# Block scales of a decoded FFN weight: the engine that multiplies them

## The chip, the cores and the metric

The kernel runs on one core of one Trainium2 chip. The metric is device time in microseconds (us). The kernel before took 1120.23 us (median of 3 runs, 1119.17 to 1120.62).

## What is computed

Two layers over x of 32 x 64 x 1024 (2048 rows of 1024), all float32:

```python
x = x + _L0_ffn_ref(_L0_cond_ref(x, L0_cond_weights, itok_B_0_15), L0_ffn_lora_A, L0_ffn_lora_B, L0_ffn_W, L0_ffn_bias, L0_ffn_lora_weights)
x = x + _L1_ffn_ref(_L1_cond_ref(x, L1_cond_A, L1_cond_B, itok_B_3_7), L1_ffn_gate_codes, ..., L1_ffn_down_scales)
```

Layer 0 picks a 64x64 channel matrix by sample, then a linear 1024x1024 with LoRA and bias. Layer 1 picks a rank 16 adapter pair by sample (8 pairs), and then runs a gated FFN with hidden size 2752, whose three weight matrices are stored as 4-bit codes with a scale for each block of 64:

```python
def dequant_nf4(codes, scales):
    out_dim, in_dim = codes.shape
    vals = NF4[codes].reshape(out_dim, in_dim // BLOCK, BLOCK)
    return (vals * scales[:, :, None]).reshape(out_dim, in_dim)
inter = jax.nn.silu(gate) * up
return jnp.einsum('bsi,hi->bsh', inter, Wd)
```

The last multiplication of `dequant_nf4`, by the block's scale, is what this document is about.

## The kernel before

**Units.** The three code matrices are cut into 65 units of 128 x 1024 codes: 21 of gate, 21 of up, 22 of down (the last one half as wide) and one tail of gate and up together. A unit n is decoded in three buffers `val` in turn. ScalarE makes eight lines (L502 the first, into `val`; L506 seven more, into a ring of five buffers), straight lines in the code. VectorE merges the seven into `val` by minimum or maximum (L666, L668), and then multiplies by the block scales (L685). These eight VectorE instructions are the steps 8n to 8n+7; 8n+7 is the scale. It raises the semaphore `scaled`, on which TensorE's `turn_unit` (L885) waits: it transposes the unit into PSUM (`ps_t`), ScalarE copies it out (gate and up into `wt`, L518; down into `wd_..._hi`, L529), and gate and up units are multiplied by the adapter A (`adapter_ga`, L893), copied out (`ga_f`, L541, semaphore `ga_evac`) and split by GpSimd into a high and a low part (`split_ga`, L417 and L419).

**Stages.** After a setup (to about 58 us) the first stage loops over 16 row tiles t: layer 0 and the adapter input Bx for the tile (L840, L851, L860, L868), with one or two units turned for each t (22 in all). The second stage loops over 6 groups of hidden chunks and, in each, over 16 slots (row tiles): down products (L972), gate and up products for the next block (L956), and up to one unit turned at the end of a slot. Group 0 has only two chunks. The result of a slot is evacuated (`staged`, L619, semaphore `out_evac`) and added to the output in memory by a GpSimd DMA (`accumulate`, L478).

**Order.** All queues are written out by hand. How many steps VectorE does in each t or slot is in `STEPS_A` and `STEPS_SLOT` (L126); ScalarE's lines run `LEAD` = 4 steps ahead. VectorE does in a slot: `product` (L786), one step, `inter_lo` (L792), `low_wd` (L703, a subtraction), the rest of the steps. GpSimd does in each t: `store_x1` of the tile before (L404), `split_ga` of the second unit of the t before, `split_bx` (L440, L442), `split_ga` of this t's first unit, `load_conds` (L398); in each slot: `split_ga` of the unit turned in the slot before, and `accumulate` of the slot before. TensorE in a t: half of `ffn_z`, `turn_x1`, `ffn_z`, `cond_y`, `adapter_ga` of the second unit of the t before, `turn_unit`, `ffn_z` and the rest. Each engine does its list strictly in order.

Of the kernel before, what the change touches and what calls it, by code (L numbers as in the profile page):

```python
# [10 lines left out]
ALU = mybir.AluOpType  # L11
# [22 lines left out]
COMBOS = len(MERGES)  # L34
# [15 lines left out]
def adaln_ffn(nc, x, cond_id, adapter_id, cond_w, lora_a, lora_b, w0, bias0, lora_w, ad_a, ad_b,  # L50
# [3 lines left out]
    P = 128  # L54
    ROWS = SAMPLES * CH
    NT = ROWS // P
    PER = P // CH
    DC = D // P
# [5 lines left out]
    BLK = D // gate_scales.shape[1]  # L64
    SB = gate_scales.shape[1]
    DSB = down_scales.shape[1]
    FULL = HID // P
    REM = HID - FULL * P
    TAIL = FULL
    NB = ROWS // HALF  # L70
    TPB = HALF // P
# [12 lines left out]
    UNITS = [(kind, c) for c in range(10) for kind in "gu"]  # L84
# [27 lines left out]
    NU = len(UNITS)  # L112
# [8 lines left out]
    STEPS = COMBOS + 1  # L121
    STEPS_SETUP = 12
    STEPS_A = [11 if t < 10 else 10 for t in range(NT)]
    LEAD = 4
    LINES_AT = [STEPS_SETUP + LEAD + sum(STEPS_A[:t]) for t in range(NT + 1)]
    STEPS_SLOT = [[4, 4, 3, 4]] + [[5, 4, 5, 4]] * (NG - 3) + [[5, 5, 5, 5], [0, 0, 0, 0]]  # L126
# [4 lines left out]
    with ExitStack() as ctx:  # L131
        def sb(name, shape, dt, where=ctx):
            return where.enter_context(nc.sbuf_tensor(name, shape, dt))

        def sem(name):
            return ctx.enter_context(nc.semaphore(name))
# [3 lines left out]
        d_scales = sb("d_scales", [P, DC, DSB], F32)  # L140
        gu_scales = sb("gu_scales", [P, FULL + 1, 2, SB], F32)
# [67 lines left out]
        gu_scales_in = sem("gu_scales_in")  # L209
        d_scales_in = sem("d_scales_in")  # L210
# [23 lines left out]
        combo = sem("combo")  # L234
        scaled = sem("scaled")
# [35 lines left out]
        def val_of(n):  # L271
            return val[:, n % 3, :]
# [11 lines left out]
        def chunk_no(g, b, k):  # L284

            return NB * GROUPS[g].start + len(GROUPS[g]) * b + k
# [90 lines left out]
        def _(pool):  # L377
# [29 lines left out]
            def split_ga(n):  # L407
                kind, c = UNITS[n]
                m, slot = GU_NO[n], c % ST
                src = ga_f[:, m % 2, :]  # L410
                if c >= ST:
                    g = GROUP_OF[c - ST]
                    pool.wait_ge(gu_mm, chunk_no(g, NB - 1, c - ST - GROUPS[g].start) + 1)
                pool.wait_ge(ga_evac, m + 1)
                if kind != "t":
                    hi, lo = st_hi[:, slot, "gu".index(kind), :], st_lo[:, slot, "gu".index(kind), :]
                    pool.tensor_tensor(hi, src, one[:, :].to_broadcast([P, P]), ALU.mult).then_inc(ga_step, 1)  # L417
                    pool.wait_ge(ga_step, m + 1)
                    pool.tensor_tensor(lo, src, hi.bitcast(F32), ALU.subtract).then_inc(ga_split, 1)  # L419
                else:  # L420

                    for half, order in enumerate(((0, 1), (1, 0))):
                        for place, part in enumerate(order):
                            ins = pool.tensor_tensor(st_hi[:, slot, half, place * REM:(place + 1) * REM],
                                                     src[:, part * REM:(part + 1) * REM],
                                                     one[:, :].to_broadcast([P, REM]), ALU.mult)
                    ins.then_inc(ga_step, 1)
                    pool.wait_ge(ga_step, m + 1)
                    for half, order in enumerate(((0, 1), (1, 0))):
                        for place, part in enumerate(order):  # L430
                            ins = pool.tensor_tensor(st_lo[:, slot, half, place * REM:(place + 1) * REM],
                                                     src[:, part * REM:(part + 1) * REM],
                                                     st_hi[:, slot, half, place * REM:(place + 1) * REM].bitcast(F32),
                                                     ALU.subtract)
                    ins.then_inc(ga_split, 1)

            def split_bx(t):
                hi, lo = bx_hi[:, t * P:(t + 1) * P], bx_lo[:, t * P:(t + 1) * P]
                pool.wait_ge(bx_masked, t + 1)
                pool.tensor_tensor(hi, bx_f[:, :], one[:, :].to_broadcast([P, P]), ALU.mult).then_inc(bx_step, 1)  # L440
                pool.wait_ge(bx_step, t + 1)
                pool.tensor_tensor(lo, bx_f[:, :], hi.bitcast(F32), ALU.subtract).then_inc(bx_split, 1)  # L442

            def is_gu(n):
                return n is not None and UNITS[n][0] != "d"
# [3 lines left out]
            for t in range(CR):  # L449
# [3 lines left out]
            pool.dma_start(d_scales[:, :, :], down_scales.rearrange("(t p) b -> p t b", p=P)  # L453
                           ).then_inc(d_scales_in, 16)
            pool.wait_ge(consts_ready, 1)
            for t in range(NT):
                if t > 0:
                    store_x1(t - 1)
                if t > 0 and is_gu(PLACE_A.get((t - 1, 1))):
                    split_ga(PLACE_A[t - 1, 1])  # L460
                if t > 0:
                    split_bx(t - 1)
                if is_gu(PLACE_A[t, 0]):
                    split_ga(PLACE_A[t, 0])
                if 1 <= t <= NT - CR:
                    load_conds(t + CR - 1)
            store_x1(NT - 1)
            split_bx(NT - 1)

            def accumulate(slot):  # L470
                t, place = slot % NT, slot % OS
                pool.wait_ge(out_evac, slot + 1)
                if slot >= NT:
                    before = slot - NT
                    pool.wait_ge(acc_out[before % OS], 16 * (before // OS + 1))
                else:
                    pool.wait_ge(x1_out[t % XS], 16 * (t // XS + 1))
                pool.dma_start(out_rows[t * P:(t + 1) * P, :], staged[:, place, :], accum_op=ALU.add  # L478
                               ).then_inc(acc_out[place], 16)

            for slot in range(NT * NG):
                if is_gu(TURN_AT.get(slot - 1)):
                    split_ga(TURN_AT[slot - 1])
                if slot > 0:
                    accumulate(slot - 1)
            accumulate(NT * NG - 1)
            for place in range(OS):
                pool.wait_ge(acc_out[place], 16 * len(range(place, NT * NG, OS)))
# [161 lines left out]
        def _(dve):  # L650
            def decode(j):

                n, op = j // STEPS, j % STEPS + 1
                if n >= NU:
                    return
                kind, c = UNITS[n]
                v = val_of(n)
                if op <= COMBOS:
                    (_, _, add), pick = MERGES[op - 1]
                    pick = ALU.max if pick == "max" else ALU.min  # L660
                    dve.wait_ge(lines, NLINES * n + op + 1)
                    if op > 1:
                        dve.wait_ge(combo, COMBOS * n + op - 1)
                    line = ring[:, (op - 1) % RING, :]
                    if add is None:
                        ins = dve.tensor_tensor(v, v, line, pick)  # L666
                    else:
                        ins = dve.scalar_tensor_tensor(out=v, in0=line, scalar=add, in1=v, op0=ALU.add, op1=pick)  # L668
                    ins.then_inc(combo, 1)
                    return  # L670
                dve.wait_ge(combo, COMBOS * (n + 1))
                if kind != "d":
                    if n == 0:
                        dve.wait_ge(gu_scales_in, 16 * 4)
                    v = v.rearrange("p (b j) -> p b j", j=BLK)
                    scales = gu_scales[:, c, "gu".find(kind) if kind != "t" else 0, :].unsqueeze(2).to_broadcast([P, SB, BLK])
                elif c == TAIL:
                    v = v.rearrange("p (t j) -> p t j", t=DC)[:, :, 0:REM]
                    scales = d_scales[:, :, DSB - 1:DSB].to_broadcast([P, DC, BLK])
                else:  # L680
                    if c == 0:
                        dve.wait_ge(d_scales_in, 16)
                    v = v.rearrange("p (t b j) -> p t b j", t=DC, j=BLK)
                    scales = d_scales[:, :, 2 * c:2 * c + 2].unsqueeze(3).to_broadcast([P, DC, 2, BLK])
                dve.tensor_tensor(v, v, scales, ALU.mult).then_inc(scaled, 1)  # L685

            def some_steps(first, count):

                for j in range(first, first + count):
                    decode(j)  # L690
# [45 lines left out]
            at = 2  # L736
# [66 lines left out]
            for g in range(NG):  # L803
                for t in range(NT):
                    slot = NT * g + t
                    works = gate_ups_at((slot - 1) // NT, (slot - 1) % NT // TPB, (slot - 1) % TPB) if slot else []
                    before = TURN_AT.get(slot - 1)
                    steps = STEPS_SLOT[g][t % TPB]
# [213 lines left out]
```

## Time and profile before

| | |
|---|---|
| median of 3 runs | 1120.23 us |
| the profiled execution | 1121.89 us, span 1120.2 us |
| TensorE busy | 1045.0 us (93%) |
| VectorE busy | 814.6 us (73%) |
| ScalarE busy | 803.5 us (72%) |
| GpSimd busy | 212.3 us (19%) |
| VectorE, merges L666 and L668 | 318.3 + 238.5 us |
| VectorE, scales L685 | 52.9 + 26.8 us |
| TensorE's granted clock, mean of the span | 0.974 |

Busy time is the time in which an engine had an instruction under way; an instruction that is held up after its start counts as busy. A wait is the idle time before an instruction and is put down to what ended it. Matmuls overlap, so a busy TensorE is not TensorE at its peak.

### The profile page before, as it was taken

How to read it: one execution, taken by the hardware profiler on the slowest of the kernel's cores; microseconds unless marked ns; L12 is line 12 of the kernel's file. 1: busy time of each engine (PE TensorE's matmuls, PEld its weight loads, DVE VectorE, ACT ScalarE, POOL GpSimd, SP SyncE). 2: the span in 40 equal slices, each digit the busy share in tenths (PEclk: the TensorE clock that was granted, in tenths of full speed). 3: DMA queues.
4: the chain of work that ended last, by engine and by line, in shares of the span. 5: the costliest groups of instructions: out<-in, count | busy, mean ns of one | idle time of the engine just before them, and what ended most of it. 6: DMA issues, size and time to landing. Idle time of an engine off the chain costs nothing.

```text
span 1120.2 us, 14573 instructions
## 1 busy us (share of the span) xinstructions
PE 1045.0 (93%) x5384; PEld 870.9 (78%) x5384; DVE 814.6 (73%) x814; ACT 803.5 (72%) x960; POOL 212.3 (19%) x285
## 2 busy tenths in 40 slices
PE   4799999999998878899999999999999999999995
PEld 3588888989897656687788888788878878777773
DVE  4778878877786888788877989788887888611110
ACT  4767777777676888888888888888888888533221
POOL 4003222232201112111131111111212111120110
PEclk9899999999999978999999999999999999999998
DMA  9635454364333365755455556546464554344444
GB/s 243 213 93 136 110 127 116 106 157 94 80 91 76 65 128 94 130 104 102 95 97 111 109 99 108 99 80 120 92 123 79 102 97 90 57 75 75 75 76 75
DMA packets 61910, 117.62 MB, mean 105 GB/s; under 512 B 5232, under 2 KB 37504, under 8 KB 61840
## 3 DMA queue, kind: packets, MB, share of 16 engines
q0 software_dynamic: 17504, 59.80, 34.4%
q1 hardware_dynamic: 43008, 55.84, 16.9%
q10 hardware_dynamic: 1328, 1.05, 0.3%
q8 instruction: 43, 0.70, 0.3%
q14 instruction: 27, 0.22, 0.1%
HBM read 57.96 MB, written 67.11 MB: 112 GB/s over the span
## 4 chain that ended last, share of the span: by engine, by line
PE 42%; DVE 27%; ACT 15%; issue 11%; SPq 2%; DMA 1%; DVEq 0%; ACTq 0%; POOL 0%
DVE val L666 16%; PE ps_z L851 10%; PE ps_z L972 9%; ACT ring L506 8%; PE ps_y L972 6%; DVE val L668 6%; PE ps_gu L956 4%; PE ps_gu L893 3%; ACT inter L605 3%; PE ps_t L893 2%; PE ps_t L885 2%; PE ps_y L840 2%; PE ps_gu L868 2%; ACT staged L619 1%; DVE inter L786 1%
## 5 line engine op out<-in xcount | busy, mean ns | idle before, releaser
L506 ACT ACTIVATE ring<-codes 128x1024 f32<-128x1024 int32 x455 | 457.8, 1055 | 118.7 <-DVE val L666 114.0
L666 DVE TENSOR_TENSOR val<-val,ring 128x1024 f32<-128x1024 f32 x260 | 318.3, 1224 | 17.1 <-issue 0.2
L668 DVE SCALAR_TENSOR_TENSOR val<-ring,val 128x1024 f32<-128x1024 f32 x195 | 238.5, 1223 | 11.0 <-ACT ring L506 3.2
L786 DVE TENSOR_TENSOR inter<-ps_gu,inter 128x512 f32<-128x512 f32 x88 | 60.8, 691 | 160.0 <-ACT inter L605 159.9
L478 POOL DMA_DIRECT2D out<-staged x96 | 82.6, 863 | 398.2 <-ACT staged L619 397.4
L605 ACT ACTIVATE inter<-ps_gu 128x512 f32<-128x512 f32 x88 | 51.6, 586 | 81.2 <-PE ps_gu L956 81.1
L851 PE MATMUL ps_z<-we_hi,y_hi 128*128 128x512 f32 x256 | 105.7, 413 | 3.6 <-DVE y_lo L711 3.6
L851 PE MATMUL ps_z<-we_hi,y_lo 128*128 128x512 f32 x256 | 101.1, 395 | 0.0
L851 PE MATMUL ps_z<-we_lo,y_hi 128*128 128x512 f32 x256 | 101.1, 395 | 0.0
L972 PE MATMUL ps_y<-wd_late_hi,in_hi 128*128 128x512 f32 (+1 forms) x256 | 82.2, 402 | 4.2 <-DVE in_lo L792 4.2
L417 POOL TENSOR_TENSOR st_hi<-ga_f,one 128x128 fp32r<-128x128 f32 x42 | 26.7, 636 | 297.2 <-ACT ga_f L541 297.0
L611 ACT ACTIVATE in_hi<-inter 128x512 fp32r<-128x512 f32 x88 | 55.6, 632 | 37.6 <-DVE inter L786 37.5
L972 PE MATMUL ps_z<-wd_late_hi,in_hi 128*128 128x512 f32 (+1 forms) x256 | 82.5, 403 | 0.0
L972 PE MATMUL ps_z<-wd_late_lo,in_hi 128*128 128x512 f32 (+1 forms) x256 | 79.2, 391 | 0.0
L972 PE MATMUL ps_y<-wd_late_lo,in_hi 128*128 128x512 f32 (+1 forms) x256 | 79.1, 390 | 0.0
L972 PE MATMUL ps_z<-wd_late_hi,in_lo 128*128 128x512 f32 (+1 forms) x256 | 78.9, 389 | 0.0
L972 PE MATMUL ps_y<-wd_late_hi,in_lo 128*128 128x512 f32 (+1 forms) x256 | 78.9, 389 | 0.0
L885 PE MATMUL ps_t<-ident,val 128*128 128x128 f32 x520 | 69.1, 276 | 9.1 <-DVE val L685 6.9
L885 PEld LDWEIGHTS ps_t<-ident,val 128*128 128x128 f32 x520 | 64.4, 174 | 15.8 <-DVE val L685 10.2
L502 ACT ACTIVATE val<-codes 128x1024 f32<-128x1024 int32 x65 | 68.4, 1053 | 10.1 <-DMA codes<-in_L_ffn_up_codes 4.3
L956 PE MATMUL ps_gu<-bx_hi,st_hi 128*128 128x512 f32 x176 | 70.9, 403 | 1.0 <-DVE inter L786 1.0
L956 PE MATMUL ps_gu<-bx_lo,st_hi 128*128 128x512 f32 x176 | 69.5, 395 | 0.0
(109 smaller groups left out, 1839.1 us busy)
## 6 DMA issues: line engine op xcount, KB each, us to landing
out<-staged POOLq DMA_DIRECT2D x96, 512.0 KB, 5.4
codes<-in_L_ffn_gate_codes SPq DMA_DIRECT2D x21, 512.0 KB, 3.9
codes<-in_L_ffn_up_codes SPq DMA_DIRECT2D x21, 512.0 KB, 3.8
codes<-in_L_ffn_down_codes SPq DMA_DIRECT2D x21, 512.0 KB, 4.7
xs<-in_x SPq DMA_DIRECT2D x16, 512.0 KB, 3.5
out<-in_L_ffn_bias SPq DMA_DIRECT2D x4, 2048.0 KB, 13.4
out<-xs POOLq DMA_DIRECT2D x16, 512.0 KB, 5.4
w_stage<-in_L_ffn_W SPq DMA_DIRECT2D x8, 512.0 KB, 9.9
```

What stands on the lines that cost most here:

```text
L478: pool.dma_start(out_rows[t * P:(t + 1) * P, :], staged[:, place, :], accum_op=ALU.add).then_inc(acc_out[place], 16)
L502: act.activation(val_of(n), codes[:, n % 2, :], ACT.Relu, bias=offset, scale=slope).then_inc(lines, 1)
L506: act.activation(ring[:, (k - 1) % RING, :], codes[:, n % 2, :], ACT.Identity, bias=offset, scale=slope).then_inc(lines, 1)
L605: act.activation(inter[0:rows, q % 2, :], ps_g[0:rows, :], ACT.Silu).then_inc(silu_ready, 1)
L666: ins = dve.tensor_tensor(v, v, line, pick)
L668: ins = dve.scalar_tensor_tensor(out=v, in0=line, scalar=add, in1=v, op0=ALU.add, op1=pick)
L786: dve.tensor_tensor(inter[0:rows, q % 2, :], ps_u[0:rows, :], inter[0:rows, q % 2, :], ALU.mult).then_inc(inter_ready, 1)
L851: ins = pe.matmul(ps_z[:, half], y[:, jc, :], w[:, jc, half], start=jc == 0 and p == 0, stop=jc == DC - 1 and p == 2)
L885: ins = pe.transpose(ps_t[:, q * P:(q + 1) * P], v[:, q, :], ident[:, :])
L893: ins = pe.matmul(ga_bank(n), ad_at[:, q, :, :].rearrange("p n r -> p (n r)"), wt[:, m % 2, q, :], start=q == 0, stop=q == DC - 1)
L956: ins = pe.matmul(ps, w[:, c % ST, m, :], v[:, cols], start=p == 0, stop=p == 2)
L972: ins = pe.matmul(ps_o[slot % 2][:, h * HALF:(h + 1) * HALF], v[0:rows, b % 2, k, s * P:(s + 1) * P], wd_of(c, w)[0:rows, h * HALF:(h + 1) ...
```

## The change

The scale of every unit is taken out of VectorE's list and put into GpSimd's. VectorE's step numbers stay as they were; step 8n+7 does nothing. GpSimd waits for the unit's seven merges (`combo`) and multiplies the same buffer in place with the same operands. `scale_units(first, count)` issues the scales whose step number lies in that stretch.

```diff
+            def scale_unit(n):
+                kind, c = UNITS[n]
+                v = val_of(n)
+                pool.wait_ge(combo, COMBOS * (n + 1))
...
+                pool.tensor_tensor(v, v, scales, ALU.mult).then_inc(scaled, 1)
+
+            def scale_units(first, count):
+
+                for n in range(NU):
+                    if first <= STEPS * n + COMBOS < first + count:
+                        scale_unit(n)
...
             pool.wait_ge(consts_ready, 1)
+            scale_units(0, STEPS_SETUP)
             for t in range(NT):
                 if t > 0:
                     store_x1(t - 1)
                 if t > 0 and is_gu(PLACE_A.get((t - 1, 1))):
                     split_ga(PLACE_A[t - 1, 1])
+                scale_units(LINES_AT[t] - LEAD, 8)
                 if t > 0:
                     split_bx(t - 1)
                 if is_gu(PLACE_A[t, 0]):
                     split_ga(PLACE_A[t, 0])
+                scale_units(LINES_AT[t] - LEAD + 8, STEPS_A[t] - 8)
                 if 1 <= t <= NT - CR:
                     load_conds(t + CR - 1)
...
+            at = LINES_AT[NT] - LEAD
             for slot in range(NT * NG):
                 if is_gu(TURN_AT.get(slot - 1)):
                     split_ga(TURN_AT[slot - 1])
                 if slot > 0:
                     accumulate(slot - 1)
+                steps = STEPS_SLOT[slot // NT][slot % TPB]
+                scale_units(at, steps)
+                at += steps
...
-                dve.wait_ge(combo, COMBOS * (n + 1))
...
-                dve.tensor_tensor(v, v, scales, ALU.mult).then_inc(scaled, 1)
```

## Rows read from the trace of the kernel before

**Rows 1.** Windows by stage: stretch, length, busy us (instructions) by engine, TensorE's granted clock, DMA.
```profile
58.00:358.00 300.00, 295.61 (x1855) 261.99 (x1854) 242.67 (x245) 212.68 (x250) 68.90 (x109) 1.00 0.45 109
358.00:455.00 97.00, 77.58 (x321) 61.77 (x320) 79.16 (x76) 79.11 (x91) 17.26 (x18) 0.84 0.56 103
455.00:975.00 520.00, 502.39 (x2499) 420.52 (x2498) 438.28 (x430) 438.93 (x533) 93.85 (x105) 0.99 0.53 99
```

**Rows 2.** Waits of TensorE, 358 to 455 us: total us, times, longest.
```profile
PE ps_t L885 <- DVE val L685: 4.4, 2, 3.2
```

**Rows 3.** Groups of instructions: busy us, mean ns of one, idle before.
```profile
L685 DVE TENSOR_TENSOR val<-val,gu_scales 128x1024 f32<-128x1024 f32 x43 | 52.9, 1230 | 0.9
L431 POOL TENSOR_TENSOR st_lo<-ga_f,st_hi 128x64 fp32r<-128x64 f32 x4 | 1.2, 322 | 0.1
```

**Rows 4.** One line's instructions, L419: duration ns min/median/max, first and last start us.
```profile
L419 POOL TENSOR_TENSOR st_lo<-ga_f,st_hi x42: 450/890/1327, 69.8 to 964.6; 128x128 fp32r<-128x128 f32 x42
```

**Rows 5.** Timeline, 83 to 86 us: start us, us, instruction, idle before and releaser.
```profile
83.83 0.40 POOL L417 TENSOR_TENSOR st_hi<-ga_f,one 128x128 fp32r<-128x128 f32 x1 [9.09 <-ACT ga_f L541]
83.86 1.45 DVE L685 TENSOR_TENSOR val<-val,gu_scales 128x1024 f32<-128x1024 f32 x1
84.31 1.32 POOL L419 TENSOR_TENSOR st_lo<-ga_f,st_hi 128x128 fp32r<-128x128 f32 x1
```

**Rows 6.** Timeline around the turn of unit 2.
```profile
80.48 1.04 PE L885 MATMUL ps_t<-ident,val 128*128 128x128 f32 x8
...
82.53 1.06 ACT L506 ACTIVATE ring<-codes 128x1024 f32<-128x1024 int32 x1 [3.72 <-DVE val L666]
...
83.49 0.26 ACT L541 ACTIVATE ga_f<-ps_gu 128x128 f32<-128x128 f32 x1
```

**Rows 7.** Timeline around the turns of units 22, 23, 24; last, a window.
```profile
369.45 1.32 POOL L442 TENSOR_TENSOR bx_lo<-bx_f,bx_hi 128x128 fp32r<-128x128 f32 x1
...
371.24 1.04 PE L885 MATMUL ps_t<-ident,val 128*128 128x128 f32 x8
...
383.22 0.86 POOL L478 DMA_DIRECT2D out<-staged  x1 [6.18 <-ACT staged L619]
...
383.56 1.97 PE L885 MATMUL ps_t<-ident,val 128*128 128x128 f32 x8 [3.24 <-DVE val L685]
...
397.59 1.10 PE L885 MATMUL ps_t<-ident,val 128*128 128x128 f32 x8 [1.20 <-DVE val L685]
...
383.00:385.00 2.00, 1.44 (x7) 1.44 (x8) 1.64 (x2) 2.00 (x3) 0.86 (x1) 0.50 0.50 34
```

**Rows 8.** Timeline around the turns of units 39, 43, 44, 61, 62, 63.
```profile
617.60 0.86 POOL L478 DMA_DIRECT2D out<-staged  x1 [8.34 <-ACT staged L619]
...
619.53 1.04 PE L885 MATMUL ps_t<-ident,val 128*128 128x128 f32 x8
...
672.33 0.86 POOL L478 DMA_DIRECT2D out<-staged  x1 [7.01 <-ACT staged L619]
...
675.19 1.04 PE L885 MATMUL ps_t<-ident,val 128*128 128x128 f32 x8
...
688.51 0.86 POOL L478 DMA_DIRECT2D out<-staged  x1 [3.06 <-ACT staged L619]
...
691.51 1.03 PE L885 MATMUL ps_t<-ident,val 128*128 128x128 f32 x8
...
928.68 1.23 DVE L685 TENSOR_TENSOR val<-val,gu_scales 128x1024 f32<-128x1024 f32 x1
...
930.14 1.05 PE L885 MATMUL ps_t<-ident,val 128*128 128x128 f32 x8
...
944.90 0.86 POOL L478 DMA_DIRECT2D out<-staged  x1 [4.44 <-ACT staged L619]
...
946.86 1.03 PE L885 MATMUL ps_t<-ident,val 128*128 128x128 f32 x8
...
957.19 1.16 PE L885 MATMUL ps_t<-ident,val 128*128 128x128 f32 x8 [2.49 <-DVE val L685]
```

More of the change, by code:

```diff
@@ L435, in split_ga @@
                     ins.then_inc(ga_split, 1)
+            def scale_unit(n):
+                kind, c = UNITS[n]
+                v = val_of(n)
+                pool.wait_ge(combo, COMBOS * (n + 1))
+                if kind != "d":
+                    if n == 0:
+                        pool.wait_ge(gu_scales_in, 16 * 4)
+                    v = v.rearrange("p (b j) -> p b j", j=BLK)
+                    scales = gu_scales[:, c, "gu".find(kind) if kind != "t" else 0, :].unsqueeze(2).to_broadcast([P, SB, BLK])
+                elif c == TAIL:
+                    v = v.rearrange("p (t j) -> p t j", t=DC)[:, :, 0:REM]
+                    scales = d_scales[:, :, DSB - 1:DSB].to_broadcast([P, DC, BLK])
+                else:
+                    if c == 0:
+                        pool.wait_ge(d_scales_in, 16)
+                    v = v.rearrange("p (t b j) -> p t b j", t=DC, j=BLK)
+                    scales = d_scales[:, :, 2 * c:2 * c + 2].unsqueeze(3).to_broadcast([P, DC, 2, BLK])
+                pool.tensor_tensor(v, v, scales, ALU.mult).then_inc(scaled, 1)
[3 more added lines that the diff above has]
+                        scale_unit(n)
             def split_bx(t):
@@ L655, in decode @@
                     return
-                kind, c = UNITS[n]
                 v = val_of(n)
@@ L669, in decode @@
                     ins.then_inc(combo, 1)
-                    return
-                dve.wait_ge(combo, COMBOS * (n + 1))
[L672 to L684, printed above, removed]
-                dve.tensor_tensor(v, v, scales, ALU.mult).then_inc(scaled, 1)
             def some_steps(first, count):
```

## The prediction

> **What bounds the kernel now.** I read four views. First, busy time by stage [rows 1]: from 58 to 358 us TensorE is busy 295.6 of 300 us, and from 455 to 975 us 502 of 520. VectorE is busy 81% and 84% of those stages. Only 358 to 455 us is different: TensorE 77.6 of 97, VectorE 79, ScalarE 79, granted clock 0.84. So in nearly nine tenths of the span TensorE sets the time, and its queue is in order: an instruction that comes late stops everything behind it, and there is hardly an idle gap later in which the loss could be made good. Second, TensorE's waits [rows 2]: it hardly waits for VectorE's scale today (4.4 us in the short stage; one more such wait in the long one). Third, what the operations cost [rows 3, 4, 5]. Fourth, and this decides, the order of time around each scale: when it ends, when TensorE turns that unit, and what GpSimd is doing then [rows 6 to 8].
>
> **What goes.** VectorE loses 65 scales: 43 x 1.230 us by the row [rows 3], and 22 more at the same duration (one of them half size), 79 us in all. Where TensorE is the bound this is worth nothing by itself. In 358 to 455 us, where merges and lines take turns, six scales of 1.22 us leave, 7.3 us; I return to them.
>
> **What comes: the operation on GpSimd.** No row shows a 128x1024 multiply there. The nearest is the subtraction of the splits, two inputs of f32: 128x64 takes 0.322 us [rows 3], 128x128 undisturbed 0.450 [rows 4]. That is 2.0 ns a column, so 0.45 + 896 x 0.0020 = 2.2 us. Bounds: no faster than VectorE's 1.22 below; eight times 0.45 = 3.6 above. I take 2.2, since both rows are the same engine and form. The Trainium skill (GPSIMD Engine Reference, 3.1 Elementwise) gives 4.497 us for an f32 tensor_tensor of 2048 columns; half of that is an estimate of 2.25, so the sum would be the same by it.
>
> **Who blocks whom.** At 83.83 GpSimd starts a 128x128 operation; VectorE's scale starts 0.03 us later and takes 1.45 instead of 1.22; GpSimd's next operation, behind it, takes 1.32 instead of 0.45 and ends with it [rows 5]. So each holds off the other when both read SBUF for two inputs. The median of 0.890 against the minimum of 0.450 says that it is usual [rows 4]. Held off for 0.23 us by 128 columns, VectorE would lose about 2.0 us to 1024 columns. A moved scale then removes 1.22 from VectorE and can put 2.0 back, net +0.8 where a merge is next, and GpSimd itself can wait up to 1.22 before it starts. The Trainium skill (SBUF, Who interferes with whom) says the same more strongly: a VectorE instruction with two SBUF inputs and a GpSimd instruction that reads SBUF exclude each other, and the second to issue waits for the whole first. By that rule nearly every scale costs VectorE; by the rows alone I charge only GpSimd's wait in the sum and leave VectorE's +0.8 to its idle time (16 to 19% of the long stages). The rule speaks against the change, and is a rival below.
>
> **What stands ahead of a scale in GpSimd's queue.** In the loop over t of the first stage the order is: store_x1(t-1), split_ga of the unit turned last, then the scales of the first eight steps. In the loop over slots it is: split_ga, accumulate(slot-1), then the scales of this slot. Both wait for ScalarE (ga_evac, out_evac). VectorE had none of these waits ahead of its scale. I placed all 65 scales by their step number (8n+7) and compared "GpSimd free or last merge done, whichever is later, plus 2.2" with the start of TensorE's turn.
>
> First stage, unit 2 [rows 6]. Its step is 23, the first of t=1, so it stands behind split_ga(1). TensorE turns it at 80.48. ga_f for unit 1 is evacuated only at 83.49 (ScalarE stands behind a ring line that waited 3.72 us), and the split ended at 85.63 [rows 5], about 84.8 once the VectorE scale that stretched it is gone, about 84.0 if the ring line also comes earlier by part of the 1.22. Plus 2.2: 86.2 to 87.0, so the turn is 5.7 to 6.5 late; I take 6.0. Everything behind it shifts. After 3.2 us of such idleness in the short stage the granted clock was 0.50, the lower of its two levels (1.2 GHz), and eight transposes took 1.97 instead of 1.04 us [rows 7, 8]; for a stall twice as long I add 1.5. Term: 7.5 (bounds 4 and 10). The other units up to 21 keep 3 us or more to spare, even beside a merge.
>
> Stage 358 to 455 [rows 7], units 22 to 24. Unit 22: GpSimd is free at 370.77, done at 373.0 at the earliest, the turn was 371.24: 1.7, with a merge in its way 2.6. Unit 23: accumulate(1) ends at 384.08, done 386.3, turn 383.56: 2.7 (VectorE then waits for a product, so no more). Unit 24: the turn already waited for the scale; the next merge starts at once, so 1.22 + 2.2 in place of 1.22: 2.2. Sum 7.5, less 0.9 where TensorE waited soon afterwards for a staged evacuation anyway: 6.6 (bounds 2 and 10).
>
> Stage 455 to 975 [rows 8]. Unit 39: accumulate ends at 618.46, plus 2.2 is 620.66, turn 619.53: 1.1, and with a merge in the way about 2.0; units 48 and 57 repeat it: 6.0. Unit 43: 673.19 + 2.2 against 675.19: 0.2, half a merge more, 0.8; 52 repeats it: 1.6. Unit 44: 689.37 + 2.2 against 691.51: 0.1 to 1.3, 0.7; 53 repeats it: 1.4. Unit 61: its last merge ends where the old scale starts, 928.68, the next merge goes first, done at 932.1, turn 930.14: 1.9. Unit 63: TensorE waited 2.49 for it already: 2.1. Unit 62, half size (about 1.2): 945.76 + 1.2 against 946.86, with a merge 1.0. Sum 14.0 (bounds 5.6 if no merge is ever in the way, 18.5 if one always is). The other 30 units from 25 on are done in time: 59 and 64 just fit, the rest even with a merge in the way.
>
> GpSimd's own queue: each scale also holds back the DMA issues behind it (store_x1, load_conds, accumulate) by 2.2 to 3.4 us. A slot is about 8 us (520 by 64) and three staged buffers follow in turn; GpSimd is idle over three quarters of the long stages [rows 1]; SP's x loads wait on x1_out with more than a t to spare. Cost 0. After 975 us no scale is left: 0.
>
> Relief: VectorE, released in the short stage, brings some lines and merges forward. Of the 7.3 us, most turns into waiting for the next product, and blocked merges take some back. I take -2 (from -7 to +3).
>
> **Sum.** 7.5 + 6.6 + 14.0 - 2 = 26. The profiled execution took 1121.9 us for a span of 1120.2; 1121.9 is 1.7 above the median of 1120.2. Added to the median: 1146 us, 2.3% slower. With the duration at 1.2 each late scale is 1.0 earlier (some 14 of them): 1132; at 3.6 they are 1.4 later: 1166.
>
> **Rivals.**
> (a) The stalls are smaller than the sum, because TensorE's later waits take them in: unit 2 at 4, the short stage 0, the long one 5.6, relief -2: 1128. For it: 17 us of idle time in the long stage. Against: those waits follow chains inside one slot (product, in_lo), which a late turn moves along with it. Time 1124 to 1130.
> (b) VectorE becomes the bound through the blocking itself: 65 x 0.8 = 52 us put on it, half of it in slots that have no idle time left, so another 26: 1172. For it: rows 5. Against: 52 us would make VectorE 867 busy, still under TensorE's 1045.
> (c) The other side: the freed VectorE decides. In 358 to 455 us ring lines and merges pass each other the turn, six scales of 1.22 leave the loop, 7.3 us, and the turns of 22 to 24 come no later: 1113. It holds if GpSimd's scale follows the last merge within 1.2 us and unit 2's wait is covered. Against: for units 22 and 23 GpSimd's previous task ends 0.5 us before the turn and 0.5 us after it [rows 7], when 2.2 us of scale are still to come.
> (d) It is hidden altogether, 1118 to 1122: stalls of some us returned by an equal relief.
>
> **Chances.** The forecast (1130 to 1166) 0.66; (a) 0.10; (b) 0.13; (c) 0.07; (d) 0.04. About 0.2% (2.2 us) is what a measurement tells from no change here. So faster 0.07, same 0.04, slower 0.89. The range of eight in ten: 1127 to 1170, which leaves out (c), (d) and the ends of (a) and (b).
>
> **What would show it.** In the changed trace: 65 GpSimd operations of 2.2 us alone, up to 3.4 beside merges; a TensorE wait of about 6 us on GpSimd's val near 80 us, and none as long later; waits of 1 to 3 us before the turns of units 22, 23, 24, 39, 43, 44, 48, 52, 53, 57, 61, 62, 63, about 28 us in all; merges of up to 3.3 us right behind a scale; VectorE's busy time above 735 us (814.6 less 79), since blocking counts as busy. I am wrong if the wait near 80 us is missing, if the scale takes under 1.5 us or over 3, if TensorE's waits for val sum to under 15 us, or if waits for in_lo or the lines grow by more than those for val, which would be (b).

## The result, and the profile after

The changed kernel takes 1155.2 us (median of 4 runs, 1154.4 to 1158.1) against 1120.4 us of the kernel before in the same comparison: ratio 1.031, interval 1.029 to 1.034. It is 34.8 us slower. The forecast was 1146 us, 26 us slower, with a range of 1127 to 1170. The profiled execution has a span of 1152.7 us. Line numbers shift: L666 is now L697, L668 is L699, L885 is L900, L792 is L807, L478 is L506; the scale on GpSimd is L454.

The page of the changed kernel: busy time, then groups of instructions (busy us, mean ns | idle before and its releasers).

```profile
PE 1050.9 (91%) x5384; PEld 871.9 (76%) x5384; DVE 783.5 (68%) x749; ACT 805.6 (70%) x960; POOL 334.5 (29%) x350
...
L697 DVE TENSOR_TENSOR val<-val,ring 128x1024 f32<-128x1024 f32 x260 | 320.1, 1231 | 17.4 <-DVE bias_x L791 0.5
L699 DVE SCALAR_TENSOR_TENSOR val<-ring,val 128x1024 f32<-128x1024 f32 x195 | 281.9, 1445 | 10.8 <-ACT ring L538 2.5
...
L454 POOL TENSOR_TENSOR val<-val,gu_scales 128x1024 f32<-128x1024 f32 x43 | 93.7, 2180 | 64.1 <-DVE val L697 57.5
```

The scale on GpSimd takes 2.2 us in the mean, as forecast, and 1.90 us where nothing is in its way. VectorE lost 79.7 us of scales, and its busy time fell by only 31.1: the 195 merges of L699 (lines 1 to 3 of a unit) grew from 238.5 to 281.9 us. Their median is still 1.224 us, but the longest is 3.342, about one merge and one whole GpSimd multiply. I call a merge held if it took over 0.5 us more than 1.224. Of the 455 merges of L697 and L699, 32 were held, by 1.4 us each in the mean and 2.1 at most. Each of them overlaps another GpSimd multiply; the other 33 multiplies held none.

```profile
L699 DVE SCALAR_TENSOR_TENSOR val<-ring,val x195: 1207/1224/3342, 14.6 to 992.3; 128x1024 f32<-128x1024 f32 x195
```

The waits of TensorE: who waited for whom, us in total, times, longest. First the changed kernel, then the same three in the kernel before. ([Rows 2] has only the short stage's part of the wait for `val`.)

```profile
PE ps_t L900 <- POOL val L454: 25.0, 11, 5.5
PE ps_t L908 <- ACT wt L550: 14.4, 11, 3.2
PE ps_y L987 <- DVE in_lo L807: 12.9, 8, 3.0
```
```profile
PE ps_t L885 <- DVE val L685: 6.9, 3, 3.2
PE ps_t L893 <- ACT wt L518: 10.0, 10, 3.2
PE ps_y L972 <- DVE in_lo L792: 7.8, 5, 2.5
```

To see where the time went, I compared the start of the same event in both traces: the evacuation of slots 0, 16 and 92 (L619 and L651). The changed kernel is 4.9 us behind at slot 0, 9.0 at slot 16 and 32.2 at slot 92. So the first stage and the setup cost 4.9 us, group 0 of the second stage (the short stage of [rows 1]) 4.1, and the long stage, in which TensorE is the bound, 23.2.

Those 23.2 us can be taken apart, because TensorE executes the same list in both traces. Between slot 16 and slot 92 it waits 7.0 us more for `val` (9.5 against 2.5), 4.9 more for `in_lo` (11.1 against 6.2) and 4.4 more for `wt` (8.4 against 4.0). Its busy time grows by 7.2 us (600.2 against 593.1). In that stretch the granted clock is 0.50 to 0.55, near the lower level, from 721 to 724, 957 to 963 and 988 to 990 us, each time beside a wait of 2.6 to 3.3 us; in the kernel before it is so once, around 902 to 904 us. The waits of 2.8 us at 927 and 3.0 us at 856 have no such stretch beside them.

Three stretches of the timeline (start us, us, instruction, idle before and releaser) show the kinds of loss. Unit 2, to be held against [rows 6]:

```profile
80.75 0.40 POOL L417 TENSOR_TENSOR st_hi<-ga_f,one 128x128 fp32r<-128x128 f32 x1 [8.20 <-ACT ga_f L573]
81.23 0.45 POOL L419 TENSOR_TENSOR st_lo<-ga_f,st_hi 128x128 fp32r<-128x128 f32 x1
81.64 1.90 POOL L454 TENSOR_TENSOR val<-val,gu_scales 128x1024 f32<-128x1024 f32 x1
83.59 1.97 PE L900 MATMUL ps_t<-ident,val 128*128 128x128 f32 x8 [5.12 <-POOL val L454]
```

The scale stands behind split_ga, and TensorE is idle for 5.1 us. The turn then takes 1.97 us instead of 1.04; from 83 to 95 us the granted clock was 0.86 of the higher level. From the turn of unit 1 to that of unit 3 the kernel lost 6.7 us. After it the delay against the kernel before stayed within 0.6 us of 4.5 to the end of the stage.

Unit 39, to be held against [rows 8] (its turn was at 619.53 there):

```profile
628.53 0.86 POOL L506 DMA_DIRECT2D out<-staged  x1 [8.34 <-ACT staged L651]
629.09 5.98 DVE L699 SCALAR_TENSOR_TENSOR val<-ring,val 128x1024 f32<-128x1024 f32 x3
629.09 2.23 POOL L454 TENSOR_TENSOR val<-val,gu_scales 128x1024 f32<-128x1024 f32 x1
631.37 1.16 PE L900 MATMUL ps_t<-ident,val 128*128 128x128 f32 x8 [0.80 <-POOL val L454]
```

GpSimd waits 8.34 us for the evacuation, then issues the DMA, then scales, and just then VectorE begins the next unit. TensorE waits only 0.80 us for the scale. VectorE's three merges take 5.98 us; in the kernel before the same three took 3.87.

Such a delay can reach TensorE a slot or two later. The third stretch shows one case. The multiply of unit 53 runs from 838.90 to 841.13 us; the second merge of the first row stands beside it and takes 3.15 us, 1.9 too long:

```profile
837.76 4.47 DVE L699 SCALAR_TENSOR_TENSOR val<-ring,val 128x1024 f32<-128x1024 f32 x2
...
853.12 0.58 ACT L637 ACTIVATE inter<-ps_gu 128x512 f32<-128x512 f32 x1
853.73 0.69 DVE L801 TENSOR_TENSOR inter<-ps_gu,inter 128x512 f32<-128x512 f32 x1 [2.56 <-ACT inter L637]
...
856.21 0.73 PE L987 MATMUL ps_y<-wd_late_hi,in_hi 128*128 128x512 f32 x2 [3.01 <-DVE in_lo L807]
```
```profile
833.35 0.73 PE L972 MATMUL ps_y<-wd_late_hi,in_hi 128*128 128x512 f32 x2 [1.09 <-DVE in_lo L792]
```

The last line is the same matmul in the kernel before. ScalarE's lines wait for merges to free the ring, and `inter` (L637) stands behind two such lines. It starts 4.0 us after the end of the gate and up products (849.12), where it started 2.1 us after them before (830.26 and 828.18). The product, `in_lo` and TensorE follow: TensorE waits 3.01 instead of 1.09 us, and those 1.9 us are the hold of one merge. In e1 below, in which no merge is held, the same matmul waits 0.65 us.

### The profile page after: what moved, and what is told of

Read it like the earlier page. It is cut to its first block, busy times and chain, and to the rows that moved or that the text cites. A ratio compares the mean times of both kernels' runs of the same rounds, so it can differ in the third digit from the quotient of the medians.

```text
span 1152.7 us, 14572 instructions
## 1 busy us (share of the span) xinstructions
PE 1050.9 (91%) x5384; PEld 871.9 (76%) x5384; DVE 783.5 (68%) x749; ACT 805.6 (70%) x960; POOL 334.5 (29%) x350
## 4 chain that ended last, share of the span: by engine, by line
PE 43%; DVE 29%; ACT 12%; issue 11%; SPq 2%; POOL 1%; DMA 1%; DVEq 0%; ACTq 0%; POOLq 0%
DVE val L697 15%; PE ps_z L866 10%; DVE val L699 9%; PE ps_z L987 8%; PE ps_y L987 7%; ACT ring L538 5%; PE ps_gu L971 4%; PE ps_t L900 3%; PE ps_gu L908 3%; ACT inter L637 2%; PE ps_t L908 2%; PE ps_y L855 2%; PE ps_gu L883 2%; DVE wd_late_lo L718 1%; DVE inter L801 1%
## 5 line engine op out<-in xcount | busy, mean ns | idle before, releaser
L697 DVE TENSOR_TENSOR val<-val,ring 128x1024 f32<-128x1024 f32 x260 | 320.1, 1231 | 17.4 <-DVE bias_x L791 0.5
L699 DVE SCALAR_TENSOR_TENSOR val<-ring,val 128x1024 f32<-128x1024 f32 x195 | 281.9, 1445 | 10.8 <-ACT ring L538 2.5
L506 POOL DMA_DIRECT2D out<-staged x96 | 82.8, 863 | 340.7 <-ACT staged L651 339.2
L454 POOL TENSOR_TENSOR val<-val,gu_scales 128x1024 f32<-128x1024 f32 x43 | 93.7, 2180 | 64.1 <-DVE val L697 57.5
L637 ACT ACTIVATE inter<-ps_gu 128x512 f32<-128x512 f32 x88 | 51.4, 584 | 83.1 <-PE ps_gu L971 82.9
L900 PE MATMUL ps_t<-ident,val 128*128 128x128 f32 x520 | 72.7, 285 | 26.8 <-POOL val L454 25.0
L900 PEld LDWEIGHTS ps_t<-ident,val 128*128 128x128 f32 x520 | 65.5, 176 | 36.8 <-POOL val L454 32.5
L807 DVE TENSOR_TENSOR in_lo<-inter,in_hi 128x512 fp32r<-128x512 f32 x88 | 60.4, 686 | 23.0 <-ACT in_hi L643 22.9
```

Source lines behind the costliest of these rows:

```text
L454: pool.tensor_tensor(v, v, scales, ALU.mult).then_inc(scaled, 1)
L637: act.activation(inter[0:rows, q % 2, :], ps_g[0:rows, :], ACT.Silu).then_inc(silu_ready, 1)
L807: dve.tensor_tensor(in_lo[0:rows, b % 2, k, :], inter[0:rows, q % 2, :], in_hi[0:rows, b % 2, k, :].bitcast(F32), ALU.subtract).then_inc(i ...
L900: ins = pe.transpose(ps_t[:, q * P:(q + 1) * P], v[:, q, :], ident[:, :])
```

## The experiments

Two theories. *Lateness*: TensorE waits because GpSimd's scale comes late (queue and 2.2 us). *Blocking*: while GpSimd multiplies, VectorE's merge stands still. The prediction charged the first and put the second to VectorE's idle time. The summary, with times against the kernel before in the same comparison:

| run | us | before | delay at slot 0, 16, 92 | held merges, slot 16 to 92: number, us |
|---|---|---|---|---|
| changed kernel | 1155.2 | 1120.4 | 4.9, 9.0, 32.2 | 18, 27.2 |
| e1 same queue, nothing read | 1127.3 | 1120.3 | 5.1, 6.5, 5.6 | 0 |
| e2 nobody scales | 1113.7 | 1120.3 | -3.6, -3.7, -7.5 | 0 |
| e3 multiply that nobody needs | 1151.1 | 1120.3 | 4.1, 7.8, 29.6 | 17, 20.9 |
| e4 unit 2 back | 1149.4 | 1120.3 | -0.7, 2.2, 27.0 | 17, 26.3 |
| e5 14 late units back | 1127.9 | 1121.0 | -2.4, -0.9, 4.6 | 9, 10.9 |
| e6 first stage only | 1121.5 | 1121.0 | -0.9, -0.6, 0.5 | 0 |
| e7 idle units | 1120.5 | 1121.0 | -2.5, -2.1, -0.9 | 0 |
| e8 scales ahead of accumulate | 1129.2 | 1121.0 | 6.2, 6.3, 5.9 | 7, 7.1 |
| e9 = e3, ahead of accumulate | 1129.9 | 1119.6 | 1.2, 2.0, 7.1 | 6, 7.7 |
| e10 ahead of accumulate and split_ga | 1123.8 | 1119.6 | -1.1, -0.9, -1.3 | 7, 7.1 |
| e11 = e8, six units back | 1119.5 | 1119.6 | -2.6, -2.4, -2.7 | 6, 5.6 |
| e12 later stages only | 1118.8 | 1119.8 | -1.8, -0.1, -1.9 | 6, 5.6 |

What the long stage loses (the third delay less the second) goes with the held time: 22 to 25 us are lost in the three runs in which 21 to 27 us are held, about 5 in e5 and e9 with 11 and 8, and at most 1.2 in all the others. So holds up to some 7 us can be covered.

In the one trace of the kernel before the turn of unit 0 came 0.9 to 3.7 us later than in every other trace, e3 and e6 included; so a part of every delay in the table, 0.9 us at least, is of that trace, and differences between two slots are safer than a single delay.

**e1: the place and the length, without the reading.** Output left without the scales.

```diff
-                pool.tensor_tensor(v, v, scales, ALU.mult).then_inc(scaled, 1)
+                for k in range(4):
+                    ...  # each waits for the one before
+                    pool.memset(scratch[:, :], 1.0).then_inc(filled, 1)      # 128x384
+                pool.wait_ge(filled, 4 * n + 4)
+                pool.memset(scratch[:, 0:1], 1.0).then_inc(scaled, 1)
```

> The scale is not computed: in its place in GpSimd's queue stand four fills of 128x384 and one of one column, some 2.0 us, that read nothing from SBUF, and then raise the signal. Lateness theory (TensorE waits because GpSimd comes late and is slow): as the changed kernel, 1150 to 1157. Blocking theory (what costs is that the multiply holds off VectorE's merges): the blocked merges are short again (L699 near 1.22 mean instead of 1.445), 1125 to 1135. My reading is that both count, about 20 us for lateness and 13 for blocking: 1142.

1127.3 us, ratio 1.006 (1.0035 to 1.008). The merges are short again:

```profile
L708 DVE SCALAR_TENSOR_TENSOR val<-ring,val 128x1024 f32<-128x1024 f32 x195 | 238.4, 1222 | 10.8 <-ACT ring L547 2.5 <-DVE val L708 0.5
```

TensorE is just as late at unit 2 (5.21 us) and waits 21.6 us for GpSimd in all, against 25.0 in the changed kernel, and still 28 us are gone, 24 of them in the long stage. Nearer to the blocking theory than I had set. One thing the run does not keep apart: fills are not held off by VectorE, so they can also end up to 1.2 us sooner.

**e2: what the relief is worth.** Output left without the scales: GpSimd's scale is left out, and `turn_unit` waits for the seventh merge.

```diff
-                pe.wait_ge(scaled, n + 1)
+                pe.wait_ge(combo, COMBOS * (n + 1))
```

> No engine multiplies by the scales; TensorE turns a unit after its seventh merge. That shows what the 79 us taken from VectorE are worth by themselves. If TensorE alone sets the time outside 358 to 455 us: 1116 to 1119 (the waits for the scales of units 22, 23, 24 and 63, 1.2 us each, go). If VectorE is the bound in the short stage as well: 1108 to 1113.

1113.7 us, ratio 0.993 (0.991 to 0.995). Between the two expectations: 79 us less on VectorE are worth 6.6 us, none of it in the short stage (-3.6 at slot 0, -3.7 at slot 16) and 3.8 in the long one. More than that this change could hardly have won.

**e3: blocking alone.** VectorE scales as before; GpSimd does this beside it, and nobody waits:

```diff
+                pool.tensor_tensor(w, ones, scales, ALU.mult).then_inc(filled, 1)   # 128x768, bf16 out
```

> VectorE multiplies the scales and signals as in the kernel before; GpSimd does, at the places of the changed kernel, a useless multiply of 128x768 (some 1.7 us, two inputs from SBUF, bf16 output to a buffer of its own) that nobody waits for. Lateness theory: 1119 to 1123, as before. Blocking theory: merges or scales behind it are held 1.5 us each, and the time rises by 10 to 25 us: 1130 to 1145.

1151.1 us, ratio 1.026 (1.023 to 1.029). No instruction depends on these multiplies, and the kernel loses 30.8 us, 21.8 between slots 16 and 92, where the changed kernel loses 23.2. Merges are held as in the changed kernel: 34 in all, 24 of them by the multiply of a unit whose multiply holds one there too (mean of the 195 merges 1437 ns, 280.2 us in all). What stands behind a useless multiply in GpSimd's queue does come later, but it does so in e1 too, where the long stage lost nothing. The time lies above my range: I had priced the blocking at 25 us at most.

**e4: unit 2 back on VectorE.** `ON_POOL` lists the units of GpSimd, each engine with its own semaphore.

```diff
+    ON_POOL = [n for n in range(65) if n != 2]
```

> Unit 2 alone is scaled by VectorE again; the other 64 by GpSimd. The wait of 5.1 us at 83.6 us and the half-clock stretch behind it go. Theory of a queue in order: minus 6 to 7, 1148 to 1149, with all later delays as they were. Rival: the time lost at unit 2 is found again later because VectorE and ScalarE had been given a lead by it: 1152 to 1155.

1149.4 us, 5.8 less than the changed kernel, whose trace had lost 6.7 there. The loss at unit 2 is a loss of queue order and is not found again; the long stage still loses 24.8.

**e5: the 14 late units back.**

```diff
+    ON_POOL = [n for n in range(65) if n not in [2, 22, 23, 24, 39, 43, 44, 48, 52, 53, 57, 61, 62, 63]]
```

> VectorE scales the 14 units that the prediction found late (2, 22 to 24, 39, 43, 44, 48, 52, 53, 57, 61 to 63); GpSimd scales the other 51. Lateness theory, as predicted: nothing is late any more, 1116 to 1122. Blocking theory: the 51 multiplies still hold merges, and with the latency run's price for blocking (28 us) scaled to 51 of 65, less some relief: 1132 to 1142.

1127.9 us, ratio 1.006 (1.004 to 1.009): between both. 14 of 65 units carried 27 of the 35 us. At first sight that is the lateness theory; but e1 had the same late turns and was as fast. Most of the late units are also units whose multiply runs beside merges: held merges in the long stage fall from 18 to 9. What is left, 7 us over 51 units, is no lateness: TensorE waited for no scale of GpSimd.

**e6 and e7: units that should cost nothing.**

```diff
+    ON_POOL = [n for n in range(22) if n != 2]                                               # e6
+    ON_POOL = [n for n in range(22) if n != 2] + [25, 26, 31, 36, 40, 45, 49, 54, 60, 64]    # e7
```

> GpSimd scales units 0, 1 and 3 to 21, which are turned in the setup and the first stage; VectorE scales unit 2 and all from 22 on. In the changed kernel no time was lost between the turns of units 4 and 21, though some 6 merges were held there; so blocking costs nothing where VectorE has idle time before TensorE needs it: 1117 to 1121. If every held merge costs: 1126 to 1132.

> As e6, and in addition units 25, 26, 31, 36, 40, 45, 49, 54, 60 and 64, after whose last merge VectorE waits for a product (operand in PSUM) instead of going on with a merge, so that GpSimd's multiply falls into idle time. Blocking theory: no merge of the later stages is held; each of the ten gives VectorE 1.2 us of idle time; 1114 to 1119, not slower than e6. Rival (any GpSimd multiply costs, wherever it stands): 4 to 7 us above e6.

Ratios 1.000 (0.999 to 1.001) and 1.000 (0.999 to 1.001). In the first stage merges are held too (13 of them in e7's trace, 14.5 us in all) and it costs nothing. The likely reason, not tested by itself, is that VectorE waits for y_hi later in most t (26 waits, 50.2 us in e7's trace), which can take the delay in. The ten units of e7, after which VectorE waits for a product, hold no merge of the later stages and win nothing either.

**e8: the scale ahead of accumulate.**

```diff
                 if is_gu(TURN_AT.get(slot - 1)):
                     split_ga(TURN_AT[slot - 1])
-                if slot > 0:
-                    accumulate(slot - 1)
                 steps = STEPS_SLOT[slot // NT][slot % TPB]
                 scale_units(at, steps)
                 at += steps
+                if slot > 0:
+                    accumulate(slot - 1)
```

> All 65 on GpSimd, but in each slot the scales stand before accumulate of the slot before, not behind it. Queue theory (accumulate in front makes units 23, 39, 43, 44, 48, 52, 53, 57 and 62 late): their waits at the turns go, some 8 us, 1145 to 1149. Blocking theory: scales start earlier, right behind the last merge and beside the same merges or more of them; at most 3 us better, 1151 to 1156.

1129.2 us, ratio 1.008 (1.005 to 1.010), far below both expectations: two lines exchanged give back 26 us. Unit 39 again, in e8:

```profile
619.77 1.90 POOL L454 TENSOR_TENSOR val<-val,gu_scales 128x1024 f32<-128x1024 f32 x1 [4.22 <-DMA out<-staged]
621.29 0.69 DVE L801 TENSOR_TENSOR inter<-ps_gu,inter 128x512 f32<-128x512 f32 x1 [1.61 <-ACT inter L637]
...
623.91 0.87 POOL L506 DMA_DIRECT2D out<-staged  x1 [2.24 <-ACT staged L651]
624.47 3.87 DVE L699 SCALAR_TENSOR_TENSOR val<-ring,val 128x1024 f32<-128x1024 f32 x3
625.83 1.04 PE L900 MATMUL ps_t<-ident,val 128*128 128x128 f32 x8
```

The multiply starts right after the last merge, runs in the 1.61 us in which VectorE waits for the product, takes 1.90 us, and is over before the next merge; TensorE turns the unit 4 us later. I had thought the scale would meet as many merges there. Between 475 and 1005 us the 105 merges of this line are busy for 156.4 us in the changed kernel, 135.4 in e8 and 127.5 in e1, in which nothing holds them: 28.9 us too much in the changed kernel and 7.9 in e8. Alone in its time the multiply takes 1.90 us, and 40 of 65 do so in e8, against 22 in the changed kernel.

**e9: the control for it.** e3's useless multiply with e8's order.

> The useless multiply of e3 (128x768, nobody waits for it, VectorE scales itself), now ahead of accumulate in each slot. If holding merges costs whenever a GpSimd multiply runs: as e3, 1147 to 1152. If it costs because accumulate in front moves the multiply from VectorE's wait for a product into the merges of the next unit: most held merges after 475 us go (28 in e3 to about 10), 1124 to 1132.

1129.9 us, ratio 1.009 (1.006 to 1.012), where e3 had 1.026. In both nobody waits for the multiply, so no lateness enters; its place alone is worth 20.5 us. Held merges in the long stage fall from 17 in e3 (not the 28 of the expectation) to 6. The exchange also makes the output DMA later; no run has that alone, but the count of held merges says where the time went.

**e10: ahead of split_ga too.** In the first stage `scale_units(LINES_AT[t] - LEAD, 8)` moves ahead of `split_ga(PLACE_A[t - 1, 1])`.

> All 65 on GpSimd, scales ahead of accumulate in each slot and, in the first stage, ahead of split_ga of the unit before. Queue theory: the stall at unit 2 and the half clock behind it (6.7 us in the changed kernel) go from e8's 1129.2: 1121 to 1124. Rival: 2.2 us of multiply and the held merges cost by themselves: 1127 or more.

1123.8 us, ratio 1.003 (1.002 to 1.005). The wait at unit 2 is gone from the trace. Against the kernel before in its own comparison e10 is 4.2 us slower and e8 8.2, so the step is worth about 4 us (5.4 as the plain difference of the two times), near the loss of unit 2. Still slower than before.

**e11 and e12: can it win?**

```diff
+    ON_POOL = [n for n in range(65) if n not in (2, 22, 23, 24, 61, 63)]     # e11, with e8's order
+    ON_POOL = [n for n in range(25, 65) if n not in (61, 63)]                # e12, with e8's order
```

> As e8 (scales ahead of accumulate), but VectorE scales the six units that TensorE still waited for (2, 22, 23, 24, 61, 63). Sum from e8's waits: 6.7 for unit 2 and its clock, 1.3 in the short stage, 1.7 for 61 and 63: 1117 to 1120. The run in which nobody scales (1113.7) is the floor. Rival: giving back six scales to VectorE costs it the lead again: 1120 to 1123, no better than before.

> Scales ahead of accumulate; GpSimd scales units 25 to 64 without 61 and 63, VectorE all the others, so that no merge of the first stage (14 us held in e8) is held. If the held merges of the first stage cost something: 1115 to 1118, better than e11. If they fall into idle time, as e6 says: 1119 to 1121, as e11 and as before.

Ratios 0.9994 (0.998 to 1.001) and 0.9988 (0.9976 to 1.0001). Neither can be told from the kernel before; of the 6.6 us that were to be had, the medians show at most 1, and the intervals allow at most 2.7.

## Why the prediction was right, and where it was not

The direction and the range held. That the sum is near is partly luck: the queue and the late units were read rightly, but most of the time was lost by a cause that the sum had put at nothing.

- **Duration of the scale, 2.2 us:** 2.18 and 2.26 mean for the two kinds of units. Undisturbed it is 1.90, less than forecast; the waits behind VectorE's instructions make up the rest.
- **Unit 2, 7.5 us:** 6.7 in the trace, 5.8 by e4 and about 4 by e10 against e8. The mechanism was right: split_ga in front, then slow matmuls.
- **Short stage, 6.6 less 2 of relief:** 4.1. The turns of units 22, 23 and 24 waited 2.29, 5.46 and 2.57 us (0, 3.24 and 1.20 before), as listed. The number is right, but its parts are not shown: e2 finds no relief in this stage, and e1, with similar waits (1.41, 5.51 and 1.65), lost only 1.4 there. Two merges were held there, for 3.2 us in all.
- **Long stage, 14.0 us from late turns:** this step failed, though the units were the right ones. The turns of 39, 44, 48, 53, 57, 61 and 63 were late (9.5 us of waits), but in e1, with the same queue and 6.2 us of such waits, the stage lost nothing against the kernel before (6.5 at slot 16, 5.6 at slot 92). Against e2, which shows the relief, the late turns are worth 2.9 us there. The rest of the stage's 23.2 us comes from the step that I had put at nothing: "leave VectorE's +0.8 to its idle time". The row was read rightly in the main (each holds the other off; but in [rows 5] GpSimd's L419 does not end with VectorE's scale, it ends 0.32 us behind it, so that most of its own 0.45 us came after). Wrong was the averaging. Half of the multiplies hold no merge at all; the other half hold one each, by 1.4 us in the mean, and 18 of these fall into the long stage, where e3 and the changed kernel lose nearly as much time as is held. That is the mechanism of rival (b), at 0.13, without its price: VectorE's busy time did not rise to 867 us but fell to 783.5.
- **Accumulate in front** was seen as the cause of lateness only. It does more: it takes the multiply out of VectorE's wait for the product, right after the last merge, and sets it beside the next unit's merges. e8 and e9 show this.
- **Relief, -2 in the short stage:** 0 there by e2, and 6.6 us over the whole kernel. In the long stage, where I had called it worth nothing, it is 3.8.
- **The signs that I had named** could not tell the two causes apart. Of those for the forecast nearly all came: a wait of 5.1 us near 80 us (though unit 23 then waited longer, 5.5), 25.0 us of waits for `val`, merges of up to 3.3 us, VectorE above 735 us. Of those against it none did: the waits for `in_lo` (+5.1) and `wt` (+4.4) grew by less than those for `val` (+18.1). Yet e1 has 21.6 us of such waits and is 28 us faster. Only taking the reading away showed the cause.

The whole in three terms, from the medians: relief -6.6 (e2), lateness 13.7 (e1 less e2), reading beside VectorE 27.9 (changed kernel less e1). Their sum is 34.9 (measured 34.8), as it must be, since each run is subtracted from the next. The last two are not quite apart (the fills of e1 are never held themselves), and by e8 both hang on the place in the queue.

Open: I followed one hold from VectorE to TensorE (856 us) and not each. Which part of the longer waits for `val` at units 61 and 63 (3.24 and 3.34 us, 0.86 and 2.23 in e1) comes from merges held earlier, and why some waits have a stretch at the lower clock beside them and others not, is open.

## What to carry to other kernels

Work moved from a busy VectorE to an idle GpSimd is not taken away for nothing while both read SBUF with two inputs: a multiply that falls beside a merge holds it, here by up to the multiply's whole length. Ask first what the relief is worth with the work left out altogether (here 6.6 us for 79.7 us of VectorE's time), and then in which gap of VectorE the GpSimd operation will fall; what stands ahead of it in GpSimd's queue decides that. Two exchanged lines were worth 26 us, more than all that leaving the scales out would bring.

## What the runs showed of the hardware

- GpSimd is not starved by back-to-back merges: it gets its turn between two of them, and the next one is then held. At 104.03 us a multiply is issued 0.16 us after a merge had begun; it takes 2.81 us instead of 1.90, and the merge after that one takes 2.74 instead of 1.22. With a multiply of 2.23 us beside them three merges took 5.98 us, and 3.87 without. The Trainium skill (SBUF — State Buffer, Who interferes with whom) calls the ports that VectorE and GpSimd share an exclusive lock, and says that a VectorE instruction with two SBUF inputs contends with a GpSimd instruction that reads. The traces agree, and show that the hold lasts for about the whole multiply in the form with a scalar as well (SCALAR_TENSOR_TENSOR, up to 3.342 us).
- A held instruction counts as busy. VectorE's busy share gives no hint of it; the mean beside the median of a line does (1445 against 1224 ns).
- Fills on GpSimd hold nothing: in e1 the merges have a mean of 1222 ns with 260 fills of 461 ns beside them.
